# MLP tiles six steps behind the attention chunks, all early dequantisation in the attention loop, transposes inside the value projections

## What is computed

```python
x = L0_attn_x
x = x + attn(layernorm(x))
x = x + ffn(layernorm(x))

# attn, for each chunk of 128 tokens and each head
decay = where(causal, exp(cla - cla.T), 0)           # cla: running sum of log(sigmoid(x @ Walpha + balpha))
att   = (q @ k.T) * beta.T * decay
y     = att @ v + (q @ state.T) * exp(cla)
state = state * exp(cla_end) + v.T @ (k * beta * exp(cla_end - cla))

# ffn
Wg, Wu, Wd = lut[codes] * scales                     # 4-bit codes, a scale for 32 values
out = (gelu_tanh(x @ Wg.T) * (x @ Wu.T)) @ Wd.T
```

## Time and profile before

| | us |
|---|---|
| median of 3 runs | 1163.4 (1162.24 to 1163.8) |
| the profiled execution, its own time | 1162.27 |
| its span, first to last instruction | 1160.5 |
| TensorE busy | 1149.0, 99% |
| VectorE busy | 718.2, 62% |
| GpSimd busy | 505.6, 44% |
| ScalarE busy | 432.3, 37% |
| TensorE's waits that the list names, n1 transposes first | 4.4, 1.8, 1.1, 0.5, 0.4 |

### The profile page before, as it was taken

How to read it: one execution, slowest core, us unless ns; L and a number is a source line. 1 busy time by engine, 2 the same in 40 slices (tenths; PEclk the granted TensorE clock), 3 DMA queues, 4 the chain that set the end, 5 groups by cost and what they waited for, 6 DMA issues and landing times.

```text
span 1160.5 us, 19350 instructions
## 1 busy us (share of the span) xinstructions
PE 1149.0 (99%) x7793; PEld 762.1 (66%) x7793; DVE 718.2 (62%) x1239; ACT 432.3 (37%) x979; POOL 505.6 (44%) x503
## 2 busy tenths in 40 slices
PE   9899999999999999999999999999999999999998
PEld 5566555566544445777777777777777777777775
DVE  7887554565666764665666566656665666555333
ACT  4343432344133232334434344434343434343332
POOL 2376332335255754335634463446353635363110
PEclk9999999999999999999999999999999999999999
DMA  8021110000010010110011001100110011000011
GB/s 298 21 84 28 32 33 10 19 19 19 8 66 1 19 37 19 37 37 19 19 37 37 19 19 38 38 19 19 37 38 19 20 37 37 19 22 26 37 38 64
DMA packets 22681, 41.93 MB, mean 36 GB/s; under 512 B 2688, under 2 KB 2752, under 8 KB 22592
## 3 DMA queue, kind: packets, MB, share of 16 engines
q1 hardware_dynamic: 22592, 40.70, 11.0%
HBM read 36.46 MB, written 4.23 MB: 35 GB/s over the span
## 4 chain that ended last, share of the span: by engine, by line
PE 96%; DVE 2%; POOL 1%; ACT 0%; issue 0%; POOLq 0%; DVEq 0%; ACTq 0%
PE ps L467 38%; PE ps L501 29%; PE ps L428 14%; PE ps L333 9%; PE ps L387 1%; PE ps L301 1%; PE ps L370 1%; PE ps L394 1%; PE ps L381 1%; PE ps L508 1%; PE ps L361 1%; POOL WR L1252 0%; DVE wf L1013 0%; DVE XT L836 0%; DVE bigA L830 0%
## 5 line engine op out<-in xcount | busy, mean ns | idle before, releaser
L501 PE MATMUL ps<-WR,ihl_s 128*128 128x512 f16 x768 | 183.6, 379 | 0.0
L501 PE MATMUL ps<-WR,vv 128*128 128x512 f16 x720 | 172.5, 379 | 0.0
L428 PE MATMUL ps<-XT,WR 128*128 128x512 f16 x768 | 170.4, 379 | 0.0
L467 PE MATMUL ps<-XT,WR 128*128 128x256 f16 x1152 | 157.1, 273 | 0.0
L467 PE MATMUL ps<-REG,WR 128*128 128x256 f16 x1152 | 157.1, 273 | 0.0
L1029 DVE TENSOR_TENSOR load<-load,ps 128x256 f32<-128x256 f32 x144 | 60.7, 421 | 144.3 <-PE ps L467 93.2
L467 PEld LDWEIGHTS ps<-REG,WR 128*128 128x128 f16 x1152 | 112.7, 98 | 33.5
L428 PEld LDWEIGHTS ps<-XT,WR 128*128 128x128 f16 x768 | 75.0, 98 | 90.3 <-DVE fw L955 0.9
L724 ACT COPY load<-ps 128x256 f32<-128x256 f32 x144 | 53.7, 373 | 211.1 <-PE ps L467 211.1
L1252 POOL TENSOR_TENSOR WR<-wf,WR 128x512 f16<-128x512 f32 x48 | 57.8, 1224 | 149.6 <-ACT WR L674 149.6
L467 PEld LDWEIGHTS ps<-XT,WR 128*128 128x128 f16 x1152 | 112.7, 98 | 13.3
(11 more groups left out here) (165 smaller groups left out, 1812.4 us busy)
## 6 DMA issues: line engine op xcount, KB each, us to landing
load<-codes SPq DMA_DIRECT2D x48, 256.0 KB
load<-scales SPq DMA_DIRECT2D x48, 256.0 KB
y<-X SPq DMA_DIRECT2D x16, 256.0 KB, 2.0
bigA<-cla SPq DMA_DIRECT2D x14, 256.0 KB, 3.2
X<-x SPq DMA_DIRECT2D x3, 1024.0 KB, 14.0
WR<-wqkv SPq DMA_DIRECT2D x2, 1024.0 KB, 10.1
X<-x SPq DMA_DIRECT2D x4, 256.0 KB, 3.9
WR<-wqkv SPq DMA_DIRECT2D x4, 256.0 KB, 4.4
```

What stands on the lines that cost most here:

```text
L428: mm = eng.matmul(bank[:, :], buf[:, wp, o + kt, 128 * j:128 * j + 128], XT[:, xp, kt, 512 * b:512 * b + 512], start=(n == 0), stop=(n == 11))
L467: mm = eng.matmul(half_bank(kind, name), w(wp, kt), x(xp, kt), start=(first and n == 0), stop=(n == 5), skip_group_check=True)
L501: mm = eng.matmul(PS[bank][:, :], ih[:, ip, 128 * tt:128 * tt + 128], buf[:, wp, 8 + j, :], start=(j == 0 and p == 0), stop=(j == end and ...
```

## The change

The MLP tiles move from four to six steps behind the chunks (`APART`), so that ten of them stand in the loop and tiles 10 and 11 behind it. Chunks 0 and 1 of the weights are no longer dequantised between the n1 transposes: the loop now does chunks 0 to 6, in steps 1, 3, 4, 5, 8, 9 and 13, and from step 4 on VectorE does the bits in the same step as the multiplications. The `down` of group 0 stand in step 10, those of group 1 two by two in steps 14 and 15, those of group 2 behind tile 12. Transposes 2 and 3 stand in the middle of the value projections 1 and 2, with five and three warm-up transposes fewer ahead. `pair` gives the banks 4 and 5 to the odd tiles from 11 on. In every step from 6 on the MLP tile comes before the n2 transpose.

```diff
-DEQUANTED = (0, 1, 5, 7, 13)
+DEQUANTED = (1, 3, 4, 5, 8, 9, 13)
+APART = 6
...
         def pair(i):
-            return (PS[2], PS[3]) if i < 12 or i % 2 else (PS[4], PS[5])
+            return (PS[4], PS[5]) if i > 10 and i % 2 else (PS[2], PS[3])
...
-            def qkv(kind, b, h):
+            def qkv(kind, b, h, halfway=lambda: None):
...
                 for kt in range(4):
+                    if kt == 2:
+                        halfway()
...
-                if i == 12:
+                if i == 11:
                     pe.wait_ge(s_attn, NT)
                     for sm5, value in banks.freed[5]:
                         pe.wait_ge(sm5, value)
-                elif i == 13:
-                    pe.wait_ge(s_inter, 12)
                 elif i >= 12:
                     pe.wait_ge(s_inter, i - 1)
...
-            warm(24)
-            for T in (0, 2):
-                turn("n1", T)
-                if T == 0:
-                    warm(3)
-                turn("n1", T + 1)
-                if T == 0:
-                    warm(10)
-                qkv("v", 0, T)
-                qkv("v", 0, T + 1)
+            warm(19)
+            turn("n1", 0)
+            warm(3)
+            turn("n1", 1)
+            warm(7)
+            qkv("v", 0, 0)
+            qkv("v", 0, 1, lambda: turn("n1", 2))
+            qkv("v", 0, 2, lambda: turn("n1", 3))
+            qkv("v", 0, 3)
...
             for T in range(NT):
-                i, fill = T - 4, fills(T)
+                i, fill = T - APART, fills(T)
                 head(T)
...
-                if T == 8:
+                if T == 10:
                     for tt in range(4):
                         down(0, tt)
-                if T >= 12:
-                    down(1, T - 12)
-                if i > 0 and i % 4:
+                if T >= 14:
+                    down(1, 2 * T - 28)
+                    down(1, 2 * T - 27)
+                if i >= 0:
                     upgate(i)
                     turn("n2", T - 1)
                     mid(T)
-                elif i >= 0:
-                    turn("n2", T - 1)
-                    mid(T)
-                    upgate(i)
...
-            for tt in range(3):
-                down(2, tt)
-            turn("n2", NT - 1)
-            down(2, 3)
             banks.ring = [0, 1, 6, 7]
-            for i in range(12, 32):
+            for i in range(NT - APART, 32):
                 upgate(i)
+                if i == 11:
+                    turn("n2", NT - 1)
+                if i == 12:
+                    for tt in range(4):
+                        down(2, tt)
...
             turn_low("n1", 0)
             weights_low(2, [2, 3])
+            stats("n1", 2)
             turn_low("n1", 1)
-            stats("n1", 2)
+            apply("n1", 2)
             stats("n1", 3)
-            apply("n1", 2)
             apply("n1", 3)
...
-                if T == 9:
-                    dq_bits(0)
-                elif T == 11:
-                    dq_finish(0)
-                elif T == NT - 1:
-                    dq_bits(1)
...
-            dq_finish(1)
             gates()
             project("k", 1, 0)
-            dq_bits(2)
-            dk = 2
+            dk = 0
             for T in range(NT):
-                i, fill = T - 4, fills(T)
+                i, fill = T - APART, fills(T)
                 weigh_keys(T)
-                if T in DEQUANTED:
+                if T in (1, 3):
                     dq_finish(dk)
                     dk += 1
                 weigh(T)
                 if T >= 1:
                     apply("n2", T - 1)
+                if T >= 4 and T in DEQUANTED:
+                    dq_bits(dk)
                 for f in fill:
                     project(*f)
+                if T >= 4 and T in DEQUANTED:
+                    dq_finish(dk)
+                    dk += 1
...
-                if T in (0, 1, 5, 9):
+                if T in (0, 2):
                     dq_bits(dk)
             apply("n2", NT - 1)
-            for tt in range(3):
-                gather(2, tt)
+            act_tile(NT - APART)
+            act_tile(NT - APART + 1)
             turn_low("n2", NT - 1)
-            gather(2, 3)
             dq_bits(7)
             dq_finish(7)
...
             load_chunk(0)
             load_chunk(1)
-            load_chunk(2)
-            load_chunk(3)
             sp.wait_ge(s_cla, 1)
```

More of the change, by code:

```diff
@@ L755, in _ @@
                     project(*f)
-                if T >= 4 and T % 4 == 0:
-                    turn("n2", T - 1)
-                if T >= 4:
-                    act_tile(T - 4)
-                if T % 4:
+                if T >= APART:
+                    act_tile(T - APART)
+                if T >= 1:
                     turn("n2", T - 1)
@@ L1083, in _ @@
                     apply("n2", T - 1)
+                if T >= 4 and T in DEQUANTED:
+                    dq_bits(dk)
                 for f in fill:
                     project(*f)
-                if T == 8:
+                if T >= 4 and T in DEQUANTED:
+                    dq_finish(dk)
+                    dk += 1
+                if T == 10:
                     for tt in range(4):
                         gather(0, tt)
-                if T >= 12:
-                    gather(1, T - 12)
-                if i > 0 and i % 4:
+                if T >= 14:
+                    gather(1, 2 * T - 28)
+                    gather(1, 2 * T - 27)
+                if i >= 0:
                     act_tile(i)
@@ L1094, in _ @@
                     mid(T)
-                elif i >= 0:
-                    turn_low("n2", T - 1)
-                    mid(T)
-                    act_tile(i)
                 else:
@@ L1116, in _ @@
                 if i == 12:
+                    for tt in range(4):
+                        gather(2, tt)
                     dq_finish(8)
@@ L1332, in _ @@
                     decay_rows(T + 2)
-                if T >= 4:
-                    inter_low(T - 4)
+                if T >= APART:
+                    inter_low(T - APART)
                 if T in DEQUANTED:
@@ L1338, in _ @@
             norm_scale("n2", NT - 1)
+            inter_low(NT - APART)
+            inter_low(NT - APART + 1)
             dequant(7)
@@ L1421, in _ @@
             load_rows(3)
-            k = 4
+            k = 2
             for T in range(NT):
```

6 lines of the change are left out of this document (removed).

## The result

The changed kernel takes **1171.9 us** (median; 1169.9 to 1172.2 over four executions) against 1163.4 us (1162.2 to 1163.8): a ratio of 1.0074, interval 1.0061 to 1.0086. It is slower, as forecast, but by 8.5 us where 3.8 were forecast, and 0.7 us above the range.

The account below looks back on a forecast made before the run. TensorE, busy 1149.0 of 1160.5 us, bounds the kernel, so only its gaps can move the time. -3.9 - 1.0 + 2.4 + 2.0 + 2.1 + 2.4 = +4.0 us against the median 1163.4: about 1167.2 us, range 1160.8 to 1171.2.

Parts of the forecast that it names:

- Part 1: Projection phase: dequantisation leaves it, so TensorE's waits for normalised rows go; 3.9 us won (3.4 to 4.4).
- part 3: Steps 0 to 2: bits of chunks 2 and 4 no longer stand there; 1.0 us won (0.5 to 1.1).
- Part 2: The start: earlier products and later copies and evacuations balance; 0 (-0.6 to +0.6).
- Part 4: Step 3: chunk 1's dequantisation ahead of `weigh` delays TensorE's local product; 2.4 us lost (1.8 to 3.5).
- Part 5: Steps 4 to 6: late GpSimd and dequantisation delay VectorE's evacuations and TensorE's bank reuse; 2.0 us lost (0.8 to 3.2).
- Part 6: Steps 13 and 14: chunk 6 ahead of the MLP tile delays transpose and `down`; 2.1 us lost (1.6 to 3.3).
- Part 7: Behind the loop: tile 12 waits for the last transpose right before it; 2.4 us lost (2.2 to 2.6).
- blocked throughout: Rival: GpSimd and VectorE block each other, losses at upper ends; +7.7 us, 1171; chance 0.10.
- Low ends: Rival: losses at their low ends, 6.4 lost, 5.5 won; +0.9 us, 1164.3, no change; chance 0.20.
- VectorE catches up: Rival: GpSimd in time in steps 2 to 5, parts 4 and 5 vanish; -0.4 or -2.5 us, 1160.9; chance 0.15.
- the clock at the start: Rival: with fewer warm-ups the first projection runs at 1.2 GHz; +5.8 us, 1169; chance 0.05.

Follow-up runs that it names:

- the run with delayed rows: Changed kernel, but in step 3 GpSimd does the decay rows of step 5 only after VectorE's weigh: 1169.8 us.
- chunks 2 and 3 behind the state: Changed kernel, old start, chunk 1 later in step 3, last transpose earlier, evacuations before bits, last chunk in step 14, chunks 2, 3 behind state update: 1159.0 us.
- the filled one: The bare run of the last pair plus 30 useless TensorE transposes in step 3's wait: 1162.9 us.
- the bare run of the last pair: Kernel of chunks 2 and 3 behind the state, with chunk 1 back in its place of the changed kernel, so step 3's wait returns: 1164.2 us.

## Why the prediction was right in direction and too small

- **Part 1 and part 3** (-3.9 and -1.0): right. By the head of step 3 the measured gain is 5.29 us for a forecast 4.9: 4.59 from the first key projection to the head of step 0, a little above part 1's range, and 1.15 in steps 0 to 2, less 0.45 that the start lost.
- **Part 2** (0): within its range. The first key projection starts at 21.97 instead of 21.52, but the old start in its place gave nothing that can be told.
- **Part 4** (+2.4): this is the step that failed, twice. The wait was sized "nearer the low end since only some of the operations meet one"; it was 3.68 us by starts (3.52 in brackets), above the upper end of 3.5. The first bit operation and the multiplications, L976 and L1008, both stood beside GpSimd, and the run with delayed rows gave 0.86 back. By the rule of the Trainium skill, "SBUF — State Buffer", section "Who interferes with whom", this wait was to lie at its upper end, and it did; I had cited the rule and sized the wait against it. (The page states full blocking of the two-port modes; for two SBUF inputs, as both these lines have, it speaks of contention with GpSimd's reads.) And the **clock** was missing. I priced a fall only at the start, as a rival of 0.05; a wait of 2 us or more in mid-kernel was priced at its length alone. Behind this one it cost 1.5 us more.
- **Part 5** (+2.0): mechanism right, 2.8 measured (1.40 + 1.34 + 0.04). `weigh_keys` of steps 4 and 5 began 5.46 and 5.47 us after the head, where 5.5 was taken. In both steps the first bit operation was blocked (1.52 for 0.68) by GpSimd's L1193; I had said that the bits that ran beside GpSimd were gone.
- **Part 6** (+2.1): 0.19 + 2.28 = 2.5; moving the chunk one step on removed the 2.28. The first bit operation was blocked here too (1.52 us).
- **Part 7** (+2.4): 2.38 in brackets, 2.57 by starts; it vanished with the transpose moved.

The steps' misses are +2.8 in part 4, 0.8, 0.4, 0.2, less 0.4 of gain: 3.7 before rounding, which is the ledger's 7.7 for my 4.0. Of part 4's 2.8, 1.3 is the wait and 1.5 the clock behind it. The last microsecond lies in the reference. My sum of 4.0 on the median of 1163.4 gives 1167.4, and I wrote 1167.2. And I took the difference of two profiled executions for that of the medians: the median of before is 1.1 us above its profiled execution, that of the changed kernel 2.0 above. The likely reason, by the mean clocks of 0.996 and 0.997 in the other three executions, is more than one fall in each of them; the kernel has three waits of over 2 us, and its profiled execution, at 0.999, one fall.

Of the rivals, *blocked throughout* (1171) was right about the wait of part 4 and comes nearest in time. That its +7.7 is the ledger's 7.7 is luck: it has no clock in it, and in steps 4 and 5, for which it took more, only the first operation was blocked. *Low ends* fell. So did *VectorE catches up*: `weigh_keys` of step 2 started 5.46 us after its head. So did the clock at the start: the first 18 projection matmuls last 3.93 us by starts, 0.218 each. The half clock that I read there from the pace of the warm-ups is in no row of the granted clock, which the trace of before records at 1.00 from 2 to 10 us.

What stays open: why the clock falls behind a given wait in one execution and not in another; and where before loses its 1.5 us in two executions of three, since its profile is of one that does not. Its longest wait after the start, 2.27 us, is a candidate that was not tried. The two kernels whose profiles have no wait of 2 us or more, chunks 2 and 3 behind the state and the filled one, were at 1.000 in all 16 executions, which fits.

## What to carry to other kernels

Price a wait of TensorE at its length and, where it is as long as those of 2.1 to 3.5 us seen here, at a further 1.5 us or so for the slower clock behind it in a part of the executions. Put work with a distant due time behind everything that the critical engine wants from that queue, for both engines that share the work: the waits of step 3, step 14 and tile 12 were worth their whole length, but in steps 3 to 6 each one mended uncovered the next lateness of the same engine. And before adding a sum to a median, see whether the profiled execution is of the median's kind.

## What the runs showed of the hardware that was not expected

- The thirteen profiles hold 22 waits of TensorE of over 2 us, and behind 8 of them the granted clock was at 0.50 for some 3 us: three of five at 3.5 us, the one of 2.66, one of six at 2.38, three of eight at 2.1, neither the one of 2.27 nor that of 2.18. No profile records a fall anywhere else. In the bare run of the last pair TensorE had been at work again for 0.9 us when the clock fell. With 30 transposes in a wait of 3.5 us the mean clock was 1.000 in eleven executions of eleven.
- So the times of one kernel come in steps: 1162.0, 1163.6 and 1165.0 us for before, with mean clocks of 1.000, 0.998 to 0.999 and 0.997; one execution of another group took 1166.4 at 0.995.
- Two multiplications of VectorE (L1008) took 1.28 us alone, 1.61 with GpSimd's rows delayed, 2.46 beside them; its first bit operation (L976) 0.68 alone, 1.41 to 1.52 beside a GpSimd operation.
